# Relation layers of a graph network: one even group of edges in sixteen filled from the table of nodes by TensorE

## The reference, cut to what matters

```
for i in range(3):
    seg = tgt * 16 + edge_type
    agg = segment_sum(x[src], seg)                  # a sum of rows for each (node, relation)
    agg = agg / clip(count of edges in seg, 1)      # a mean
    x_new = einsum('nrd,rdo->no', agg, W[i]) + x @ root[i] + bias[i]
    x = relu(x_new) if i < 2 else x_new
```

## Time and profile before

| | us |
|---|---|
| median of three runs | 3432.25 |
| the profiled execution's own time | 3401.57 |
| its span | 3399.8 |
| PE busy (24551 matmuls) | 2653.2 |
| DVE busy | 2193.1 |
| ACT busy | 1323.8 |
| POOL busy (1212 gathers of 958 ns among it) | 1219.4 |
| share of the chain that ended last that is transfers by gathers | 15% |

### The profile page before, as it was taken

How to read it: one execution, slowest core, us unless ns; L and a number is a source line. 1 busy time by engine, 2 the same in 40 slices (tenths; PEclk the granted TensorE clock), 3 DMA queues, 4 the chain that set the end, 5 groups by cost and what they waited for, 6 DMA issues and landing times.

```text
span 3399.8 us, 80962 instructions
## 1 busy us (share of the span) xinstructions
PE 2653.2 (78%) x24551; PEld 1772.8 (52%) x24552; DVE 2193.1 (65%) x7930; ACT 1323.8 (39%) x2937; POOL 1219.4 (36%) x1269
## 2 busy tenths in 40 slices
PE   3337777768899995888888888888888888888887
PEld 1323333335456683555555555555555555555555
DVE  6689999976453454666566556656666556566665
ACT  0149999973222212333333333333333333333332
POOL 3020000000000002555555545555555455555554
PEclk9569999999999997999999999999999999999999
DMA  0011111121101026444444444444444444454442
GB/s 26 20 58 43 46 43 46 43 68 47 32 24 45 8 78 208 121 124 122 121 118 121 124 123 118 121 122 123 120 120 122 124 119 122 121 123 121 120 121 80
DMA packets 228329, 314.99 MB, mean 93 GB/s; under 512 B 41665, under 2 KB 201004, under 8 KB 227708
## 3 DMA queue, kind: packets, MB, share of 16 engines
q1 hardware_dynamic: 187548, 227.23, 24.9%
q0 software_dynamic: 40672, 86.39, 9.0%
HBM read 268.23 MB, written 45.23 MB: 92 GB/s over the span
## 4 chain that ended last, share of the span: by engine, by line
PE 25%; DMA 16%; issue 10%; POOL 3%; DVE 3%; another core or an unknown queue 3%; DVEq 0%; POOLq 0%; ACT 0%; SPq 0%; ACTq 0%
DMA arena<-pair,arena 15%; PE psum L2308 8%; PE psum L2321 7%; PE psum L2332 4%; PE psum L2285 4%; POOL arena L2218 3%; DVE arena L2501 1%; PE psum L2298 1%; DVE arena L2507 1%; DVE arena L2497 1%; DVE arena L2537 0%; DMA arena<-rows 0%; PE psum L2386 0%; DMA pair<-arena 0%
## 5 line engine op out<-in xcount | busy, mean ns | idle before, releaser
L2218 POOL DMA_INDIRECT arena<-pair,arena x1212 | 1161.1, 958 | 906.7 <-DMA h<-h 381.9
L2507 DVE SCALAR_TENSOR_TENSOR arena<-psum,arena,work 128x304 f32<-128x304 f32 x606 | 429.9, 710 | 718.7 <-DMA h<-h 469.5
L2442 ACT ACTIVATE arena<-psum 128x512 f16<-128x512 f32 x303 | 180.7, 597 | 1108.3 <-remote 763.1
L2321 PE MATMUL psum<-arena 128*128 128x304 f16 x3939 | 566.1, 293 | 18.9 <-issue 17.8
L2308 PE MATMUL psum<-arena 128*128 128x304 f16 x2424 | 370.6, 296 | 207.3 <-DMA arena<-pair,arena 162.2
L2501 DVE TENSOR_SCALAR arena<-arena 128x304 f16<-128x304 f16 x2121 | 483.1, 300 | 0.0
L2321 PEld LDWEIGHTS psum<-arena 128*128 128x128 f16 x3939 | 360.9, 98 | 193.5 <-issue 81.7
L2285 PE MATMUL psum<-arena 128*32 128x256 f16 x7272 | 367.1, 277 | 117.9 <-issue 109.1
L2439 ACT ACTIVATE arena<-psum 128x1024 f16<-128x1024 f32 x303 | 308.9, 1019 | 227.8 <-DMA h<-h 134.7
L2308 PEld LDWEIGHTS psum<-arena 128*128 128x128 f16 x2424 | 213.7, 98 | 346.7 <-issue 234.4
L2332 PE MATMUL psum<-arena 128*128 128x152 f32 (+1 forms) x2496 | 378.0, 297 | 6.5 <-DVE arena L2507 6.5
(11 more groups left out here) (289 smaller groups left out, 3217.6 us busy)
## 6 DMA issues: line engine op xcount, KB each, us to landing
work<-inverse SPq DMA_DIRECT2D x606, 152.0 KB
arena<-pull SPq DMA_DIRECT2D x303, 224.0 KB
pull<-rows SPq DMA_DIRECT2D x101, 224.0 KB
arena<-pair,arena POOLq DMA_INDIRECT x1212
h<-work SPq DMA_DIRECT2D x8, 640.0 KB
h<-h POOLq DMA_DIRECT2D x8, 640.0 KB, 6.9
pair<-arena SPq DMA_DIRECT2D x12, 256.0 KB
x_pad<-arena SPq DMA_DIRECT2D x1, 1600.0 KB, 5.3
```

Of the source, the lines that this page charges most:

```text
L2218: e.indirect_dma_start(out=t.msg[:, j, k].rearrange("p h f -> p (h f)"), out_offset=None, in_=d[f"pair_{l}"].rearrange("n h f -> n (h f)") ...
L2321: m = e.matmul(p.psum[:, 1, 0:KEYS], t.smsg[:, j % 2, tile, half, :], t.soh[:, j % 2, tile, :], start=(tile == 0 and half == 0), stop=(til ...
L2507: e.scalar_tensor_tensor(t.agg[h % 2][:, :, k % BATCH, :], p.psum[:, k % 2, 0:KEYS].rearrange("p (r w) -> p r w", r=REL), t.back[:, l:l + ...
```

## The change

Pair 5 of each turn (`TWIN = 5`, one in `EVERY = 8`) has its even group filled as odd groups are. That is 12 groups for each layer (`TWINS`), 36 fills in three layers; the pulls become `PULLS` = 113.

```
+EVERY, TWIN = 8, 5
+TWINS = PAIRS // EVERY
+PULLS = PAIRS + TWINS
@@ build_adjacency, vector: 12 further rounds behind the 101
+        def twin_sources(r):
+            par, first = r % 2, ((r - PAIRS) * EVERY + TWIN) * 2 * GT
+            e.wait_ge(s_gm, r)
+            e.tensor_copy(t.stage[:, par, 0, 0:GT], t.columns[:, 0, first:first + GT]).then_inc(s_tc, 1)
+            e.tensor_copy(t.stage[:, par, :, GT:], t.slot_key[:, :, r * GT:(r + 1) * GT]).then_inc(s_tc, 1)
+            e.wait_ge(s_tc, (r - PAIRS) * 2 + 2)
+            for k in range(GT):
+                e.tensor_scalar(t.oh_s[par][:, GT + k, :], t.iota_h[:, 0:P], t.stage[:, par, 0, k:k + 1], None,
+                                ALU.is_equal).then_inc(s_th, 1)
+        for r in range(PAIRS, PULLS):
+            if r + 1 < PULLS:
+                twin_sources(r + 1)
+            slot_keys(r - 1, (r - 1) % 2)
+            if r + 1 < PULLS:
+                twin_hots(r + 1)
+            ones(r)
@@ build_adjacency, tensor
+        for r in range(PAIRS, PULLS):
+            slot_keys(r - 1, (r - 1) % 2)
+            e.wait_ge(s_th, (r - PAIRS + 1) * GT)
+            place(r, r % 2, [t.twin_slot[r % 2][:, k, :] for k in range(GT)])
@@ slots: every step over the odd groups is done for the twelve twins too
+        sides = (odd, 0, PAIRS), (twin, PAIRS, PULLS)
@@ relations, sync: one buffer for a twin's pull
+                    if j == TWIN:
+                        e.wait_ge(s_ga, twin_fill(l, i) * FILLS + FILLS)
+                        twin_pull(bass.ds(i + (PAIRS + 1), 1))
@@ relations, gpsimd
             for j in pairs:
+                if j == TWIN:
+                    continue
@@ relations, tensor
+            def twin_pair(turn):
+                blocks_of(turn, TWIN, 0, 4)
+                for tile in range(SLOT_TILES):
+                    twin(turn, tile)
+                apply(turn, 0, BATCH, TWIN % HALF)
+                rest_of(turn, TWIN, PIECES * (TWIN - HALF - 1))
+                blocks_of(turn, TWIN + 1, 0, 4)
+                for tile in range(SLOT_TILES):
+                    filled(turn, TWIN, tile)
+                rest_of(turn, TWIN + 1, PIECES * (TWIN - HALF))
             def pairs_of(turn, h, first, pairs, fills):
                 for j in range(h * HALF, h * HALF + pairs):
+                    if j == TWIN:
+                        twin_pair(turn)
+                        continue
+                    if fills and j + 1 == TWIN:
                         for c in range(4):
-                            quad(turn, j + 1, c)
+                            twin_quad(turn, c)
@@ relations, scalar
             def takes(turn, later, more):
                 for j in range(TP):
+                    if j + 1 == TWIN:
+                        twin_take(turn)
                     take(turn, j + 1)
@@ relations, vector, in onehots
+            if twin:
+                for c in range(SLOT_TILES):
+                    e.tensor_scalar(t.twin_oh[:, c, :], t.iota[:, 0:KEYS], t.twin_keys[:, c:c + 1], None,
+                                    ALU.is_equal).then_inc(s_oh, 1)
```

More of the change, by code:

```diff
@@ L982, in turn, with place @@
                 m.then_inc(s_mm, 1)
-        def place(r, par):
+        def place(r, par, hots):
             e.wait_ge(s_slot, r * GT + GT)
@@ L1837, in rank_memory @@
     c = p.carve(t.free)
-    n = PAIRS * BLOCKS
+    n = PULLS * BLOCKS
     t.ohb = c(GT * n // 2, F16).rearrange("p (k g b) -> p k g b", k=GT, b=BLOCKS)
     t.sized = [c(ACROSS * BLOCKS) for _ in range(2)]
-    t.place, t.base, t.over, t.tmp = (c(PAIRS * GT) for _ in range(4))
-    t.code, t.bits, t.first = (c(PAIRS * GT, I32) for _ in range(3))
-    t.start, t.piece = c(PAIRS * GT), c(PAIRS * GT)
+    t.place, t.base, t.over, t.tmp = (c(PULLS * GT) for _ in range(4))
+    t.code, t.bits, t.first = (c(PULLS * GT, I32) for _ in range(3))
+    t.start, t.piece = c(PULLS * GT), c(PULLS * GT)
     t.lower, t.every, t.none, t.raised = (c(P // 2, F16) for _ in range(4))
@@ L2113, in uses, with fill, twin_fill, hots @@
         return len(range(slot, PAIRS, G_AHEAD))
+    def fill(l, turn, j):
+        return turn * (TP + 1) + (l * PULLS + j + (1 if j >= TWIN else 0))
+    def twin_fill(l, turn):
+        return turn * (TP + 1) + (l * PULLS + TWIN)
+    def hots(l, turn, j):
+        return turn * HOT_TURN + (l * HOTS + j * HOT_PAIR + (SLOT_TILES - GT if j > TWIN else 0))
     @block.sync
@@ L2235, in _ @@
         regs = [e.alloc_register(f"spare{k}") for k in range(TP * PIECES)]
+        twin_regs = [e.alloc_register(f"twin_spare{k}") for k in range(PIECES)]
         e.sem_inc(s_mm, MM0)
@@ L2348, in pairs_of @@
                         bounds(l, j)
-                    if fills:
+                    if fills and j + 1 == TWIN:
                         for c in range(4, 6):
-                            quad(turn, j + 1, c)
-                        spares(j + 1, PIECES * (j - first))
+                            twin_quad(turn, c)
+                        spares(t.twin_pull, twin_regs)
+                    elif fills:
+                        rest_of(turn, j + 1, PIECES * (j - first))
                     for tile in range(SLOT_TILES):
@@ L2360, in _ @@
                 e.wait_ge(s_p0, 16)
-            for c in range(6):
-                quad(0, 0, c)
-            spares(0, 0)
+            blocks_of(0, 0, 0, 4)
+            rest_of(0, 0, 0)
             pairs_of(0, 0, -1, HALF, True)
@@ L2457, in takes @@
                 next_pick(turn, 1, later)
+                if more:
+                    twin_pick(turn + 1)
             rooted(l)
```

192 lines of the change are left out of this document (131 added, 61 removed).

## The result

The changed kernel takes 3740.78 us (median of 4 runs, 3735.66 to 3755.28); before takes 3433.81 on the same chip (4 runs). The ratio is 1.0902 [1.0889, 1.0916]: 307 us slower, where I forecast 39 faster. The profiled execution took 3735.66 us.

What follows compares the result with a forecast made beforehand. Runs of four gathers were taken to hold the pace, 6.62 us a pair. Gathers -86, twelve rounds +42 and ranking +5 gave -39 us: 3393 us as a median, range 3335 to 3482 (forecast's own 3340 to 3447).

Steps and rivals of the forecast that it cites:

- SP and DMA: Loads in each turn: one 224 KB pull replaces four 64 KB gathers, plus new key and register loads; claimed to cost nothing.
- The gathers (-86 us): Relation layers: 144 of 1212 gathers go, shortening pairs 3 and 4; 2.4 us less in each of 36 turns.
- from R(2) to R(4): Stretch between the moments the odd sums of pairs 2 and 4 are out; POOL's gather runs there were to be at most two.
- my own sign of being wrong: Pair 5's stretch taking 8 us or more would mean the twin is dearer than its matmuls.
- lost again: Rival: gathers hold the pace elsewhere and the freed time is lost in the turn; +47 us, 3479 us, chance 0.18.
- my second rival: Rival: TensorE is the bound and the twin lengthens its work; +120 us, 3552 us, chance 0.12.
- the twin's 2.0 us of matmuls: Added TensorE work in pair 5, counted in its 6.6 us; 73 us if its cover by the gathers is gone.
- The ranking: One-time DVE work: larger block one-hots and rank columns; +5 us, range 3 to 8.
- the twelve rounds: Twelve more rounds of pull matrices behind the last round, 3.5 us each; +42 us, range 40 to 61.
- Three more one-hots: DVE work added for the twin, 0.7 us; claimed to cost nothing, or 0.7 if the slack of 0.8 is gone.
- the pull behind SP's wait: SP waits for the twin's fill ahead of pair 5's, with inverse counts queued behind; claimed to cost nothing.
- The port rule: DVE and GpSimd share a port pair, so added one-hots could delay a gather; at most 25 us, not counted.

Runs made afterwards that it cites:

- split_load: The kernel before with TensorE's load of 24 spare registers split into two of 12, the second half a turn later: 3435.73 us, 1.0000 of before.
- half_gathers: The kernel before with the gathers of pairs 1, 3, 5 and 7 of each turn left out (stale table used): 3196.71 us, 0.9303 of before.
- after_tuned: The changed kernel with aligned register tables, the 24-register load split, the twin's three-register load moved to just ahead of its spare matmuls: 3509.16 us, 1.0213 of before.
- before_ruler: The kernel before with eighteen extra register loads on TensorE's queue ahead of the relation layers: 3183.73 us, one execution.
- after_aligned: The changed kernel with padding that puts both register tables back at their old offset modulo 64 bytes: 3246.60 us, 1.0232 of before.
- after_again: The changed kernel itself, unaltered, run on a chip where before takes 3183.11 us: 3482.48 us, 1.0947 of before.
- shift_spare: The kernel before with only the spare table (TensorE's load) moved by 10 words: 3337.36 us, 1.0513 of before.
- shift_gbase: The kernel before with only the table of window bases (DVE's and SP's loads) moved by 10 words: 3190.15 us, 1.0047 of before.
- before_shifted: The kernel before with both register tables moved by 10 words, nothing else changed: 3341.04 us, 1.0531 of before.
- before_shift_16_bytes: The kernel before with both register tables moved by 4 words (16 bytes): 3164.95 us, 0.9969 of before.

## Why the prediction was wrong

How long each pair takes, from the start of the odd mean of pair j-1 to that of pair j, mean of all turns, by j modulo 8 (worked out from the 606 starts of the mean in each trace, pairs 3 to 98 of each layer, 36 values to a column); the twin is made for pair 5, and the additions stand ahead of the odd means of pairs 3 and 7:

```
                              0     1     2     3     4     5     6     7    turn
kind 1, before              6.45  6.58  6.51  6.89  6.49  6.58  6.66  6.91   53.1
               after        5.55  6.45  6.69  7.22 11.05  8.86  6.40  8.51   60.7
kind 1, split_load          6.70  6.68  6.65  6.81  6.70  6.71  6.74  6.81   53.8
             half_gathers   5.59  5.00  6.65  6.01  5.80  4.97  6.91  6.15   47.1
             after_tuned    5.86  6.44  6.67  7.29  5.35  8.71  6.00  7.88   54.2
kind 2, before_ruler        5.56  5.59  6.12  6.07  5.78  5.81  5.97  6.17   47.1
            after_aligned   5.61  5.58  6.17  5.93  6.01  6.27  5.88  5.99   47.4
            after_again     4.77  6.04  5.88  6.83 11.48  6.27  5.83  6.92   54.0
            shift_spare     5.57  5.53  6.05  6.07 10.66  5.16  6.47  6.00   51.5
            shift_gbase     4.69  6.08  5.78  6.76  5.04  6.14  5.65  7.18   47.3
```

**The step that failed** is the last sentence of SP and DMA: "The new two-instruction loads of keys and registers, once a turn: nothing." I costed the loads that were added and not those that were there, whose operand the change moved. Once a turn TensorE's own queue stands still 4.05 us longer for the old load and 0.77 for the new one, and then works 5.2 us at half its clock, which by the rows above makes the sums and the apply 1.00 and 1.03 us longer. It is pair 4 that pays: 11.05 for 6.49. DVE's load, 1.25 us longer and ahead of the additions, delays pairs 3 and 7 (5.93 to 6.83, 5.99 to 6.92 between after_aligned and after_again). In shift_gbase the next pair gives that back (pairs 0 and 4 fall to 4.69 and 5.04), so it costs 15 us.

The new load of three registers was not nothing either: it is the gap of 1.01 us in after_aligned, though pair 4 is only 0.23 longer there (6.01 for 5.78).

Why is the loss 227 us in the changed kernel and 166 in before_shifted, which has the same two loads? In the changed kernel pair 4 pays 5.47 us (11.48 for 6.01) and pair 5 gives nothing back; in before_shifted pair 4 pays 4.24 (10.02 for the 5.78 of before_ruler) and pair 5 gives back 0.65 (5.16 for 5.81). Most of the 61 us between them is clock. Over the relation layers the granted clock is 0.94 in after_again against 0.99 in after_aligned, and 0.96 in before_shifted against 0.99 in before_ruler: some 104 and 60 us lost, an estimate that takes TensorE as always busy. TensorE's gap is 5.06 us long in the one and 4.10 in the other; whether that is what keeps the clock low for longer is open.

The Trainium skill (Runtime: NRT & Kernel Launch, section Instruction fetch mechanics) puts a load of registers at about 200 ns a register, even in bulk; the page has loads from HBM in mind. From SBUF the rows here give 236 ns off a 16-byte boundary, near to it, and 67 ns on one, a third of it; for this case the measurement decides. The Trainium skill (SBUF — State Buffer, section Operand start alignment) lets an operand start at any multiple of its element's size, and says that this is about legality and not speed. The runs here agree that such a start works, and show what it costs.

**The gathers (-86 us)** failed as well, by a smaller amount. Between first and last mean after_tuned takes 2105.0 us (1382.2 to 3487.2) and before_split_load on the same chip 2081.9 (1331.5 to 3413.4): +23 where the step says -86. With it the sum closes: -39 + 109 (from -86 to +23) + 237 (the tables) = +307. Two parts of the step are wrong. The first is pair 5, at 6.6 in my sum and 8.71 measured. POOL, TensorE, ACT and DVE of after_tuned in that pair:

```profile
2397.32 0.94 POOL L2300 DMA_INDIRECT arena<-pair,arena  x1 [0.30 <-issue]
...
2399.82 0.74 DVE L2662 SCALAR_TENSOR_TENSOR arena<-psum,arena,work 128x304 f32<-128x304 f32 x1 [0.34 <-PE psum L2426]
2400.26 1.86 PE L2413 MATMUL psum<-arena 128*128 128x304 f16 x13
2400.57 1.02 POOL L2300 DMA_INDIRECT arena<-pair,arena  x1 [2.31 <-PE psum L2426]
...
2404.65 0.95 POOL L2300 DMA_INDIRECT arena<-pair,arena  x1 [0.30 <-issue]
2404.91 1.20 PE L2426 MATMUL psum<-arena 128*128 128x304 f16 x6 [0.43 <-issue]
...
2406.58 0.60 ACT L2577 ACTIVATE arena<-psum 128x512 f16<-128x512 f32 x1 [4.95 <-remote]
...
2408.54 0.74 DVE L2662 SCALAR_TENSOR_TENSOR arena<-psum,arena,work 128x304 f32<-128x304 f32 x1 [4.91 <-PE psum L2426]
```

A run of four gathers lies from 2400.57 to 2405.60. ACT's second copy of pair 5's fill waits for TensorE's fills of that same pair, and comes 0.98 us behind the run: late, as results behind a run of four are on this kind. In every other pair this copy is wanted one pair later; in the twin's order `filled(5)` wants it at once, so the 13 sums stop halfway and the mean comes at 2408.54. I had costed ACT's first copy and not the second. The second wrong part is "from R(2) to R(4) no run is longer than two". POOL lagged, so in this turn the run from 2386.00 to 2390.69, the four gathers of pair 4, still had four, and the even mean behind it started at 2391.85. So it was in 22 of the 36 turns. Pairs 3 and 4 together took 12.64 us (5.23 + 5.63 = 10.86 forecast, 13.51 in before_split_load). So the direction was right for the two together. Pairs 0 and 6 gained too (6.70 to 5.86, 6.74 to 6.00), and all of it went into the twin's own pair and into pair 7 (6.81 to 7.88). Pair 5 passes my own sign of being wrong, 8 us: on kind 1 the twin is dearer than its matmuls. Of the rivals, "lost again" gives +47 and comes nearest to the aligned kernel's 1.0213, 73 us.

**Other points.** That runs of four gathers set the pace was right for kind 1 (0.9303) and false on kind 2, where a pair takes 5.9 us. There my second rival's bound, TensorE and its waits, is the better picture, but the twin's 2.0 us of matmuls cost only 0.5 in pair 5 and 0.3 a turn., on which I rested it in part, could not have told: those sums ended 1.96 us behind the second gather, and not beside one. The ranking (5, measured 4.4) and the twelve rounds (42, measured 43) were right. Three more one-hots and the pull behind SP's wait were tested by no run of their own; with the twin's matmuls and the new load they share the 25 us of after_aligned's layers. The port rule that I weighed, at most 25 us, was tested by no run by itself; on kind 2 pair 5's gathers move the time by at most 0.5%. My forecast's own range does not follow from its bounds, which give 3335 to 3454 and not 3340 to 3447; no reading hangs on it.

## What to carry to other kernels

When a change makes an array bigger, list what stands behind it in SBUF and who loads registers from there: a long register load off a 16-byte boundary costs 236 ns a register here instead of 67, on the queue of the engine that waits. A few words of padding are the fix: six here, and by before_shift_16_bytes two would do, which no run tried. A profile's rows of register loads show at once whether it is needed. A load at the top of a loop is free while the matmuls handed over before it last (1.62 us beside 13 sums of 1.85); what is longer idles TensorE, and behind 5 us of that the matmuls ran at the low clock. And before trusting a pace read from one trace, ask whether it is the kernel's or that of the chip it ran on.

## What the runs showed of the hardware that I had not expected

- Registers loaded from SBUF: 24 in 1.62 us, 12 in 0.85, 8 in 0.60 at a multiple of 16 bytes; 24 in 5.67, 8 in 1.85 at 8 bytes beyond; 15 in 3.58 from an odd word; 3 in 0.77, whatever their place. The engine's queue hands out nothing meanwhile; what it handed out before runs on.
- Two kinds of chip run the same program at 3167 to 3183 us and at 3434 to 3437. They agree up to the relation layers (first mean at 1330.2 and 1330.9 us). In these, one of them holds back TensorE's results behind runs of four gathers, and the other does not. Why is open, and also whether it is the chip.
- Behind a gap of 5.06 us TensorE's granted clock was 0.50 for the next 5.2 us, and the sums and the apply in them took 2.03 us longer than at full clock.
